# First expert's first weight quarters loaded into buffers that the last passes leave free, counting matmuls of the routing placed later, bias split and maxima placed earlier

## The reference

```python
x = x + _L0_xcond_ref(_layernorm(x), ctx_2048, ctx_2048, itok_B_779_1933)   # attention over channels
x = x + _L0_ffn_ref(_layernorm(x), gate_w, w1, b1, w2, b2, wd, wu, sw1, sb1, sw2, sb2, swd, swu)

# attention: per head, s = SCALE * log(length of the batch)
attn = softmax(s * einsum('bhdq,bhdk->bhqk', qh, kh)); out = einsum('bhqk,bhdk->bhdq', attn, vh)

# feed-forward: E = 8 experts, 2 chosen per token, cap = 320 tokens per expert and choice
top_p, top_i = top_k(softmax(xt @ gate_w), 2)
for k in range(2):
    pos = position of the token among those that chose expert e as choice k;  keep = pos < cap
    h = gelu(buf @ w1 + b1);  y = h @ w2 + b2 + gelu(buf @ wd) @ wu
    out += y[e, pos] * keep * top_p[:, k]
out += 0.2 * (gelu(xt @ sw1 + sb1) @ sw2 + sb2 + gelu(xt @ swd) @ swu)   # shared expert
```

## Time and profile before

| what | value |
|---|---|
| median of 3 runs | 1408.8 us (1408.75 to 1411.6) |
| the profiled execution's own time | 1401.34 us |
| its span, first to last instruction | 1399.5 us |
| PE busy in the span | 1346.4 us (96%) |
| DVE, ACT, POOL busy | 812.6, 687.5, 249.1 us |
| mean granted clock of PE | 0.992 |

### The profile page before, as it was taken

How to read it: one execution, slowest core, us unless ns; L and a number is a source line. 1 busy time by engine, 2 the same in 40 slices (tenths; PEclk the granted TensorE clock), 3 DMA queues, 4 the chain that set the end, 5 groups by cost and what they waited for, 6 DMA issues and landing times.

```text
span 1399.5 us, 27035 instructions
## 1 busy us (share of the span) xinstructions
PE 1346.4 (96%) x11193; PEld 967.1 (69%) x11211; DVE 812.6 (58%) x1313; ACT 687.5 (49%) x1023; POOL 249.1 (18%) x219
## 2 busy tenths in 40 slices
PE   5788999999999999999999999999999999999997
PEld 2152737364645555384788889998888888888895
DVE  7776778686978777762743625536255362452620
ACT  5866666667575756561523524335243342432511
POOL 4720010000000000452201304013030030300202
PEclk9999999999999999999999999999999999999999
DMA  9613131413131222118735665466454565553402
GB/s 273 203 37 100 52 93 39 113 39 106 46 96 49 84 54 92 24 25 213 233 102 124 168 131 157 126 149 164 130 157 109 134 178 131 151 132 99 99 6 38
DMA packets 136731, 155.89 MB, mean 111 GB/s; under 512 B 59049, under 2 KB 79673, under 8 KB 136610
## 3 DMA queue, kind: packets, MB, share of 16 engines
q1 hardware_dynamic: 124322, 128.97, 31.7%
q0 software_dynamic: 12288, 25.21, 9.6%
HBM read 109.47 MB, written 34.15 MB: 103 GB/s over the span
## 4 chain that ended last, share of the span: by engine, by line
PE 81%; DVE 8%; ACT 5%; issue 2%; DMA 1%; SPq 1%; POOL 1%; POOLq 0%; ACTq 0%; DVEq 0%
PE banks L1722 25%; PE banks L1752 24%; PE banks L1641 9%; PE banks L1659 6%; PE banks L1581 4%; PE banks L1561 3%; PE banks L1529 3%; DVE rowmax L1192 2%; DVE late_stage L1213 2%; ACT hidden L982 2%; PE banks L1774 1%; ACT QS L969 1%; PE banks L1615 1%; PE banks L1590 1%; SPq L801 1%
## 5 line engine op out<-in xcount | busy, mean ns | idle before, releaser
L1752 PE MATMUL banks<-hidden,w2h 128*128 128x0 bf16 x2048 | 313.0, 273 | 0.0
L982 ACT ACTIVATE hidden<-banks,scales 128x512 f32<-128x512 f32 x256 | 170.1, 686 | 111.8 <-PE banks L1561 92.4
L1752 PEld LDWEIGHTS banks<-hidden,w2h 128*128 128x128 bf16 x2048 | 198.4, 98 | 25.7
L1752 PE MATMUL banks<-hidden,w2l 128*128 128x0 bf16 x1024 | 195.7, 273 | 0.0
L1192 DVE TENSOR_REDUCE rowmax<-banks 128x1 f32<-128x512 f32 x256 | 172.7, 684 | 37.3 <-PE banks L1529 35.4
L1343 DVE TENSOR_TENSOR w1l<-stage,w1h 128x2048 bf16<-128x2048 f32 x32 | 73.4, 2292 | 199.7 <-ACT w1h L1058 199.7
L1075 ACT ACTIVATE hf<-banks,b1cols 128x640 f32<-128x640 f32 x128 | 101.7, 794 | 178.0 <-PE banks L1722 172.3
L1659 PE MATMUL banks<-w2h,hidden 128*128 128x512 bf16 x512 | 185.4, 381 | 0.0
L1082 ACT ACTIVATE yT<-banks 128x640 f32<-128x640 f32 (+1 forms) x32 | 22.1, 691 | 270.1 <-PE banks L1752 270.1
L1722 PE MATMUL banks<-eth,w1h 128*128 128x0 bf16 x1024 | 136.2, 276 | 3.2 <-ACT lowf L1065 3.2
L1722 PE MATMUL banks<-etl,w1h 128*128 128x0 bf16 x1024 | 136.8, 277 | 0.0
(11 more groups left out here) (194 smaller groups left out, 1963.3 us busy)
## 6 DMA issues: line engine op xcount, KB each, us to landing
stage<-in_L_ffn_w SPq DMA_DIRECT2D x64, 1024.0 KB, 5.5
split_parts<-hidden SPq DMA_DIRECT2D x16, 512.0 KB, 2.9
QS<-split_parts SPq DMA_DIRECT2D x48, 128.0 KB, 3.1
KS<-split_parts SPq DMA_DIRECT2D x48, 128.0 KB, 3.4
xin<-in_x SPq DMA_DIRECT2D x16, 256.0 KB, 3.6
cin<-in_ctx SPq DMA_DIRECT2D x16, 256.0 KB, 3.1
out_rows<-xin SPq DMA_DIRECT2D x16, 256.0 KB, 2.0
normed_rows<-x2r SPq DMA_DIRECT2D x16, 256.0 KB, 2.8
```

The costliest lines, as they stand in the source:

```text
L982: ac.activation(prob[n % NPH], bank(score_bank[unit]), ACT.Exp, scale=scales[:, g // 2:g // 2 + 1]).then_inc(s_exp, 1)
L1752: issued = mm(half_of(bank(b0 + j)).shape_from_register(bank_cols(e, j)), w[:, fb, rows], half_of(a[:, fb, :], j).shape_from_register(slot ...
```

## The change

Five edits. (1) In the last up pass a unit "first_stages" has SP load the first three weight quarters of expert 0 into three other places (`first_stages`): the place of `split`, `late_stage`, and the upper half of the probabilities. e_split 0 to 2 then split from there, and load only quarters 3 and 4; e_split 3 moves behind e_rank and wu. (2) The ten transposing transfers of expert 0 come first in `first_weights`, and the first of them waits until quarters 0 and 1 are split, since etl lies over `late_stage`. (3) "place" comes 13 units later in part 0 and 5 later in part 1. (4) In window 0 "parts" and "rows" of group 1 come inside group 0's steps, and "b2_parts" at step 0 of group 1 in place of step 9. (5) ACT's split of shared quarters 4 and 6 waits for 4 and 8 low pieces in place of 16, and POOL's low pieces of quarters 4 on wait for the earlier ones that they overwrite.

```diff
--- before.py
+++ after.py
@@ -156,7 +156,9 @@
         for k in range(19 + (EARLY_GROUPS if part == 0 else GROUPS - EARLY_GROUPS)):
             add("route", part, k)
             yield
-        yield
+        for _ in range(6 if part else 14):
+            yield
         add("place", part)
         for k in range(10):
             add("slot", part, k)
@@ -204,10 +206,10 @@
                     next(score, None)
                     if k == 0 and w == 0 and i < 5:
                         next(score, None)
-                if k == 0 and w:
-                    if i == LATE + 2:
+                if k == 0:
+                    if i == (LATE + 2 if w else UNITS - 3):
                         add("parts", g + 1)
-                    elif i > LATE + 3:
+                    elif i > (LATE + 3 if w else UNITS - 3):
                         next(rows, None)
                 if w == 0:
                     if k * UNITS + i in QUARTERS:
@@ -216,7 +218,7 @@
                         low_piece()
                     if k == 0 and i == 13:
                         add("wd", E)
-                    if k == 1 and i == 9:
+                    if k == 1 and i == 0:
                         add("b2_parts")
                     if k == 1 and i == UNITS - 3:
                         add("fills", 1)
@@ -233,8 +235,6 @@
                     value_step(*divmod(g * QT + i // GH - 1, QT))
                 if k == 1 and i == ONES and g - 1 in SUMMED:
                     add("ones", g - 1)
-            if k == 0 and w == 0:
-                add("parts", 1)
             for _ in rows if k == 0 else ():
                 pass
             one_of(side, 99)
@@ -267,6 +267,8 @@
                 ready_sums(b * UNITS + UNITS)
             if n == 1:
                 value_step(b, QT - 1)
+            if not more and n == 6:
+                add("first_stages")
             if n == ONES - 1 and b in SUMMED:
                 add("ones", b)
             if more and n in (2, 3):
@@ -379,13 +381,12 @@
 
     def first_weights():
         add("wd", 0)
-        for q in range(4):
+        for c in range(CH):
+            add("turn_x", 0, c)
+        for q in range(NST):
             for _ in range(6):
                 yield
             add("e_split", q)
-            if q == 0:
-                for c in range(CH):
-                    add("turn_x", 0, c)
 
     def last_downs():
         for p in range(PASSES - 2, PASSES):
@@ -399,6 +400,8 @@
     for e in range(E):
         add("e_rank", e)
         add("wu", e)
+        if e == 0:
+            add("e_split", NST)
         for fb in range(FB):
             if fb % 4 == 0:
                 add("e_split", 8 * e + 4 + fb // 4)
@@ -556,6 +559,10 @@
 
         offset[0] = routing_start
         stage = [at(f"stage{i}", [P, 2048], F32, 4) for i in range(NST)]
+        first_stages = [hidden[:, 2 * FB * PASS + 2 * NPH * L:][:, 0:4096].bitcast(F32), late_stage[:, :],
+                        hidden[:, 2 * FB * PASS + NPH * L:][:, 0:4096].bitcast(F32)]
         eth = [at(f"eth{i}", [P, KB, SLOTS], BF16, 2) for i in range(2)]
         etl = [at(f"etl{i}", [P, KB, SLOTS], BF16, 2) for i in range(2)]
         yT = at("yT", [P, KB, SLOTS], F32, 4)
@@ -681,6 +688,9 @@
         def low_no(e):
             return PASSES + e + 1
 
+        def stage_of(j):
+            return first_stages[j] if j < NST else stage[j % NST][:, :]
         def split_no(j):
 
             return 8 + j + 1
@@ -688,6 +698,13 @@
 
         def sync_program(sp):
             dma = nc.sync.dma_start
+            def load_quarter(n):
+                e, q = divmod(n, 8)
+                src = (w1[e].rearrange("(k p) f -> p k f", p=P)[:, :, q * 512:q * 512 + 512] if q < 4
+                       else w2[e].rearrange("(k p) d -> p k d", p=P)[:, (q - 4) * 4:(q - 4) * 4 + 4, :])
+                dma(stage_of(n).rearrange("p (a w) -> p a w", w=512), src).then_inc(s_stage[n % NST], 16)
             for unit in plan:
                 kind = unit[0]
                 if kind == "load":
@@ -793,6 +810,10 @@
                         table.rearrange("(e p c) two -> p e (c two)", p=P, c=CH)).then_inc(s_table, 16)
                 elif kind == "turn_x":
                     _, e, c = unit
+                    if e == 0 and c == 0:
+                        sp.wait_ge(s_whi, split_no(1))
+                        sp.wait_ge(s_wlo, 2)
                     sp.wait_ge(s_gather[c], 16 * (e + 1))
                     if e >= 2 and c == 0:
 
@@ -801,16 +822,17 @@
                         dma(turned[:, :, c * P:c * P + P], xg[:, c, a * D:a * D + D], transpose=True).then_inc(s_turned, 16)
                 elif kind == "e_split":
                     j = unit[1]
-                    for n in range(3) if j == 0 else range(j + 2, j + 3):
-                        if n >= 64:
-                            continue
-                        if n >= NST:
-                            sp.wait_ge(s_whi, split_no(n - NST))
-                            sp.wait_ge(s_wlo, n - NST + 1)
-                        e, q = divmod(n, 8)
-                        src = (w1[e].rearrange("(k p) f -> p k f", p=P)[:, :, q * 512:q * 512 + 512] if q < 4
-                               else w2[e].rearrange("(k p) d -> p k d", p=P)[:, (q - 4) * 4:(q - 4) * 4 + 4, :])
-                        dma(stage[n % NST][:, :].rearrange("p (a w) -> p a w", w=512), src).then_inc(s_stage[n % NST], 16)
+                    n = j + NST - 1
+                    if j and n < 8 * E:
+                        sp.wait_ge(s_whi, split_no(n - NST))
+                        sp.wait_ge(s_wlo, n - NST + 1)
+                        load_quarter(n)
+                elif kind == "first_stages":
+                    sp.wait_ge(s_ones, len(SUMMED))
+                    sp.wait_ge(s_pv, GROUPS * QT)
+                    for n in range(NST):
+                        load_quarter(n)
             n = GROUPS + (E - 1) * CH
             for r in range(3):
                 sp.wait_ge(s_yst[r], yst_before(n, r))
@@ -871,6 +893,9 @@
                     dst_hi, dst_lo = (w1h, w1l) if n < 4 else (w2h, w2l)
                     cols = (slice(None), slice(q * 512, q * 512 + 512)) if n < 4 else (slice(q * 4, q * 4 + 4), slice(None))
                     pool.wait_ge(s_whi, n + 1)
+                    if n >= 4:
+                        pool.wait_ge(s_wlog, 12 if n < 6 else 16)
                     whole, hi, lo = (hstage[n].rearrange("p (a w) -> p a w", w=512), dst_hi[:, cols[0], cols[1]],
                                      dst_lo[:, cols[0], cols[1]])
                     gp.tensor_tensor(lo[:, a], whole[:, a], hi[:, a], ALU.subtract).then_inc(s_wlog, 1)
@@ -1002,8 +1027,9 @@
                     q = n % 4
                     dst = w1h[:, :, q * 512:q * 512 + 512] if n < 4 else w2h[:, q * 4:q * 4 + 4, :]
                     act.wait_ge(s_hstage[n], 16)
-                    if n == 4:
-                        act.wait_ge(s_wlog, 16)
+                    if n in (4, 6):
+                        act.wait_ge(s_wlog, 4 if n == 4 else 8)
                     ac.activation(dst, hstage[n].rearrange("p (a w) -> p a w", w=512), ACT.Copy).then_inc(s_whi, 1)
                 elif kind == "rank":
                     p = unit[1]
@@ -1055,7 +1081,7 @@
                         if q == 4:
                             act.wait_ge(s_down, down_no(PASSES - 1) if e == 0 else e_down_no(e - 1, KB - 1))
                         dst = w2h[:, (q - 4) * 4:(q - 4) * 4 + 4, :]
-                    ac.activation(dst, stage[j % NST][:, :].rearrange("p (a w) -> p a w", w=512), ACT.Copy).then_inc(s_whi, 1)
+                    ac.activation(dst, stage_of(j).rearrange("p (a w) -> p a w", w=512), ACT.Copy).then_inc(s_whi, 1)
                 elif kind == "e_rank":
                     e = unit[1]
                     act.wait_ge(s_rank, PASSES + e + 1)
@@ -1340,7 +1366,7 @@
                     dve.wait_ge(s_whi, split_no(j))
                     lo, hi = ((w1l[:, :, q * 512:q * 512 + 512], w1h[:, :, q * 512:q * 512 + 512]) if q < 4
                               else (w2l[:, (q - 4) * 4:(q - 4) * 4 + 4, :], w2h[:, (q - 4) * 4:(q - 4) * 4 + 4, :]))
-                    dv.tensor_tensor(lo, stage[j % NST][:, :].rearrange("p (a w) -> p a w", w=512), hi, ALU.subtract).then_inc(s_wlo, 1)
+                    dv.tensor_tensor(lo, stage_of(j).rearrange("p (a w) -> p a w", w=512), hi, ALU.subtract).then_inc(s_wlo, 1)
                 elif kind in ("route", "slot"):
                     part, k = unit[1], unit[2]
                     first, last = (0, EARLY_GROUPS) if part == 0 else (EARLY_GROUPS, GROUPS)
```

## The result

The changed kernel takes 1420.47 us (median of 4 runs, 1419.66 to 1422.39), the kernel before beside it 1408.78 us (4 runs, 1408.46 to 1411.6): a ratio of 1.0071, 95% interval 1.0049 to 1.0093. It is 0.7% slower, where I forecast 0.7% faster. The profiled execution has a span of 1417.8 us, 18.3 more than that of before.

The account below looks back on a forecast made before the run. PE, busy almost throughout from 142 to 564 us and after 672 us, was taken as the bound, keeping gains won earlier. Window 0 -4.8, part 0 -1.3 and experts' entry -4.1 gave -10.2 us: 1398.6 us, range 1393.2 to 1406.5.

Parts of the forecast that it names:

- Window 0: -4.8 forecast: Window 0: moving the bias instructions gives ACT back 5.2 us of idle time, less 0.4 us lost: -4.8 us.
- "0.4 us lost" at the row copies: Window 0: earlier "rows" hold PE's values back, so ACT's four row copies start at 51.5 us, not 51.11.
- the bound that I named: Window 0's slow bound, -2.5 us: late values drop PE to its lower clock level and take 1.9 us more.
- "not won" for quarter 4's split: Window 0: quarter 4's split no longer waits 1.63 us for POOL, but this brings no gain.
- Part 0: -1.3 forecast: Part 0's counting: the 4.6 us stall goes, 2.4 us return as another stall, half a clock loss remains: -1.3 us.
- The clock term: Part 0's counting: after the new 2.4 us stall, half of a 1.7 us loss to PE's lower clock was assumed.
- The way into the experts: -4.1 forecast: Entry to the experts: e_rank's 3.22 us stall and 1.67 us slow clock go, a 1.9 us wait comes: -4.1 us.
- The ten transfers: Way into the experts: ten transposing transfers at the first one's 1.31 us take 13.1 us in place of 14.05.
- the 2.7: Way into the experts: quarter 4 of the weights lands some 2.7 us after quarter 3, at 663.7 us.
- the tail gives nothing: Rival, chance 0.15: the transposing transfers start only at 646.5 us or later, so the total is -6.1: 1402.7 us.
- My rival of the scatters: Rival, chance 0.07: POOL's 18 scatters slow to 2.27 us each beside DVE, ending 15.1 us late: 1413.7 us.
- The sum's base: Whole kernel: -10.2 us on the profiled 1401.3, with the median's 7.5 us above it kept as a shift: 1398.6 us.

Follow-up runs that it names:

- e17: The changed kernel as it is, measured a third time: 1402.65 us, ratio 1.0015 to the kernel before.
- e5: The changed kernel as it is, run again: 1422.65 us, ratio 1.0058 to the kernel before.
- e7: Kernel before with only b2_parts moved to the start of group 1: 1410.39 us, ratio 0.9978.
- e4: Changed kernel with group 1's "parts" and "rows" (maxima) back where the kernel before has them: 1399.66 us, ratio 1.0011.
- e8: e4 with quarter 3's load issued ahead of the ten transposing transfers: 1415.25 us, ratio 1.0015 to the kernel before.
- e12: e11 and e8 together, with the maxima as in the kernel before: 1410.48 us, ratio 0.9992 to the kernel before.
- e18: Changed kernel with maxima and both counting places as before, and quarter 3's load ahead of the transposing transfers: 1393.64 us, ratio 0.996 to the kernel before.
- e10: Kernel before with at most two scatters under way: 1405.85 us, ratio 0.9964.
- e2: Changed kernel with both parts' counting matmuls placed as in the kernel before: 1400.2 us, ratio 0.9996 to the kernel before.
- e6: The kernel before as it is, profiled again beside e5: one run of 1415.78 us.
- e9: Kernel before without part 0's series of 15 scatters behind 602 us: 1399.17 us, ratio 0.9913.
- e11: Changed kernel with only part 0's counting matmuls back at their old place: 1416.25 us, ratio 1.0032 to the kernel before.
- e13: Kernel before with only the change's early loads and its order of loads and transposing transfers: 1400.54 us, ratio 1.0005.
- e14: e7 with part 1's counting matmuls six steps behind the counting: 1398.68 us, ratio 0.9988 to the kernel before.
- e15: e7 and e10 together, on the kernel before: 1405.3 us, ratio 1.003.
- e1: Changed kernel with the three early loads issued at the start of first_weights, ahead of the transposing transfers: 1405.93 us, ratio 1.0048 to the kernel before.
- e16: Changed kernel with e10's limit of two scatters under way: 1417.3 us, ratio 1.0119 to the kernel before.
- e3: Changed kernel with the three early loads seven up blocks later: 1401.52 us, ratio 1.0012 to the kernel before.
- sets A, D and E: Groups of runs on one chip each, beside the kernel before (1399.83, 1400.88, 1399.57 us): e1 to e4; e13 to e16; e17 and e18.
- sets B and C: Groups of runs on one chip each, beside the kernel before (1413.98 and 1411.99 us): e5 to e8; e9 to e12.

## Why the prediction was wrong, by its own steps

Without standstills the change costs 2.1 us (0.15% of 1399.57, e17; the medians differ by 3.1), where I forecast a gain of 10.2; with them it costs 8.7 us (e5) to 11.7.

**Window 0: -4.8 forecast, about 0 found.** b2_parts gains what it moves: the rank activation comes at 75.0 on average in three traces with this edit alone (73.97 to 75.59), and at 77.3 in five with the old window (75.58 to 78.86), -2.3 us, and e7 is 3.1 us faster. With the whole edit it is 77.2 in eight traces (75.97 to 78.16). The step that failed is the sum's "0.4 us lost" at the row copies: it is 2.0 us in the changed kernel. There the late values run at the lower clock (48.3 to 51.7), which is the bound that I named; up to 80 us the low clock adds up to 10.2 us in both traces.

With b2_parts and the split waits, but the old maxima (e4, e8, e12, e18), the rank activation comes at 76.5, and the row copies at 52.9 to 54.0, just as late. So undoing the maxima does not bring the 2 us back, and I overlooked why: without the wait for all 16 pieces ACT splits quarter 4 earlier, and POOL's low pieces of it then lie beside DVE's low part of `wd`. These are the three DVE instructions before and in e4, then e4's POOL and PE:

```profile
48.31 0.69 DVE L1281 TENSOR_TENSOR wdl<-wdf,wdh 128x128 bf16<-128x128 f32 x3
```

```profile
48.46 3.46 DVE L1309 TENSOR_TENSOR wdl<-wdf,wdh 128x128 bf16<-128x128 f32 x3
```

```profile
47.19 4.58 POOL L903 TENSOR_TENSOR w2l<-xt_stage,w2h 128x512 bf16<-128x512 f32 x4
```

```profile
52.35 0.62 PE L1571 MATMUL banks<-identb,MS 128*32 128x128 bf16 x16 [5.60 <-DVE MS L1229]
```

All twelve traces with the split waits have these three instructions at 2.5 to 3.6 us, all eight without at 0.7. With the old maxima, MS stands behind them and PE waits for it; with the new ones MS is ahead of them, and the values are late instead. So the part that I put down as "not won" for quarter 4's split shows as a loss: 1.5 us between 75.0 and 76.5 on average, and the two groups don't overlap (73.97 to 75.59, 75.67 to 78.05). The maxima's share, 0.7 us between 76.5 and 77.2, is not shown, since executions of the same window 0 differ by up to 3.3 us at this mark (e10 has 3.4 us of low clock up to 80 us and 75.58, before 10.2 us and 78.86). No run leaves out the split waits alone. Two slips of the sum are small beside this: the 0.2 us allowed for POOL is not in the -4.8, and the bound with 1.9 us more is -2.9, not -2.5.

**Part 0: -1.3 forecast, 0 found.** Stall gone, stall of 2.46 us in its place, to 0.1 us as forecast. The clock term was the doubtful half. Twelve traces have the old place and its 2.9 us stall: the clock fell behind it in seven (before, e2, e6, e9, e10, e11, e13), not in five (e7, e12, e14, e15, e18). Eight have the new place: it fell behind the 2.46 us stall in five (after, e1, e5, e16, e17), not in e3, e4, e8. This is e7's stall, and a window across the very stretch that ran at 0.56 before:

```profile
563.96 0.27 PE L1675 MATMUL banks<-onehotb,before 128*128 128x224 bf16 x1 [2.93 <-DVE earlier L1400]
```

```profile
563.90:567.80 3.90, 3.84 (x21) 1.72 (x25) 3.23 (x9) 2.06 (x3) 0.00 (x0) 1.00 0.00 0
```

From the first block of one up pass, at about 512 us, to that of the next, at about 590, it is 77.5 us in four traces of the old order that fell (before, e6, e9, e13), 77.3 to 78.0 in the changed kernel's three, 75.8 in e7 (old, no fall) and 75.8 in e4 (new, no fall): the edit gives nothing in either case. The 1.7 us go with window 0 instead: the clock stayed up in all seven traces that have b2_parts early and the old maxima, and fell in twelve of the other thirteen (not in e3). So much earlier work can only act here by shifting times; by what rule, I can't tell.

**The way into the experts: -4.1 forecast, +2.0 found** (tail 772.8 against 769.4, less the 1.4 us in the up pass). The wait for e_rank went and the last scatter and the table's load came 2.3 us later against the last gelu, where I had 2.0. The first transposing transfer was even earlier than I had it (15.9 us behind the last gelu; by my sum 645.15 - 628.7 = 16.5). Two terms were mis-sized. The ten transfers took 658.79 - 643.43 = 15.4 us, not 13.1 (14.8 in the first trace): I had priced them all at the first one's duration. And quarter 4 came 5.6 us behind quarter 3, not 2.7, though both were issued together. No row stood behind the 2.7: where the kernel before loads three quarters together, ACT's splits start 4.1 and 4.6 us apart (643.05, 647.11, 651.73). Other transfers run beside quarter 4 (the wu loads, a store of output rows, quarter 5); which of them takes the time isn't separated. So PE waited 5.78 us, not 1.9, and the lower clock that I had put down as won came back behind it (668.7 to 675.6). The rival "the tail gives nothing" had the right place; it was worse than nothing, because part 1's later counting (+2.4 behind the last gelu, e14) and the early loads (0, e13) together cost 3.4: with loads and transfers behind one another in SP's queue, each delay of the transfers is handed on to quarter 4. Where there are standstills the tail loses 6.6 us (e5 against e6): PE itself stands still while DVE makes part 1's slots, so in the kernel before the last scatter is issued 2.0 us ahead of the last gelu, and in the changed one 3.5 us behind it. About 3.1 of the 6.6 us are the small standstill ahead of e6's mark.

**The standstill** was in no rival. It isn't of the change: e6 has it. It hangs on the series of scatters (e9), and goes when at most two are under way (e10). Of the change is that the series is three scatters longer (16.0 us of standstill in e5, 12.7 in e11). My rival of the scatters had the right engine and the wrong price: they did not get slower. Nearly all of the 18 take 0.97 to 0.99 us, 1.28 us apart, beside DVE in e17 too (the longest there is 1.10). By the rule of the Trainium skill that I weighed there ("SBUF — State Buffer", Reading the diagram) I had all of them long; no trace here shows that for the casts of the up pass, which take 0.2 to 0.5 us each. That each of them would make a scatter long was my own reading, and it failed.

**The sum's base.** I put the profiled execution's 1401.3 beside the median of 1408.8 as a shift of 7.5 us that would stay. It was two kinds of execution: the profile of before had no standstill, and sets without have medians of 1399.6 to 1400.9, sets with them 1412.0 to 1414.0. Single executions of the kernel before lie between 1395.1 and 1405.5 us in sets A, D and E, and between 1408.2 and 1417.0 in B and C. The four of the first measurement (1408.46 to 1411.6) lie in the second range, so that they had a standstill is likely; no trace of them shows it.

The 1.0071 of the first measurement is thus, most likely, the tail's loss and the longer series in executions with a standstill; the exact shares there can't be told, since the one trace of the kernel before that belongs to it has no standstill.

## What to carry to other kernels

A moved load or wait should be priced on what is behind it in its queue: where transfers and loads stand in one queue, take the spread of the durations, not the first, and the landing of the second load from a row where it is seen. Edits that each have a reason should run apart: b2_parts alone was worth 0.22%, and with the early loads and quarter 3 ahead of the transfers 0.4% (e18, in which the split waits still stand; without them it was not run); bundled with the maxima, the split waits and part 1's place it was lost. A wait that is taken away starts other work sooner: look at what that work then runs beside. And where the profiled execution and the median differ by more than runs scatter, find out what the other executions look like before adding to either.

## What the hardware showed that I had not expected

- Beside a series of indirect scatters of 128 small rows, 1.28 us apart, PE's semaphore updates came up to 14 us late, with DMA nearly idle (0.02 busy from 612 to 628 us in the changed kernel). It appears in whole sets of runs and not in others, on the same chip too. The traces of sets B and C, and the first one of the changed kernel, also hold fewer events of scatters that landed: 97 behind 600 us in the changed kernel, 118 in e6, but 288 to 352 in the unpaced kernels of the other sets. Of landing events of all transfers they hold 7,715 to 7,985, the others 8,559 to 8,571. This goes with the set and not with the long standstill: e9 and e10 lack the events too. Whether the recording of events has a part in it, or what else differs between the sets, no run here tells.
- Three DVE subtractions of 128x128 took 0.69 us in all, and 3.46 us with POOL's subtractions of 128x512 beside them (before, e4).
- The same stall of 2.9 us is followed by a 3.4 us stretch at the lower clock in seven traces (6.8 us around it in e10) and by none in five; 3.4 us of it make a difference of 1.7 us.
- Two 1 MB loads issued together behind transposing transfers landed 5.6 us apart (e17); by the starts of ACT's splits it is 3.3 to 5.6 us in the ten traces that have this order.
